# Grouped attention: 1280 of a unit's 1857 softmax columns traded by DMA instead of 1024, with new orders of step on all engines

## The reference

```
q = (latents @ Wq).reshape(b, q_len, N_KV_HEADS, N_GROUPS, HEAD_DIM)     # 32 heads of 128, 4 key heads
k = (hidden_states @ Wk).reshape(b, kv_len, N_KV_HEADS, HEAD_DIM)        # kv_len = 256 + 1601 = 1857
v = (hidden_states @ Wv).reshape(b, kv_len, N_KV_HEADS, HEAD_DIM)
scores = jnp.einsum('bqhgd,bkhd->bhgqk', q, k) * scale
attn = jax.nn.softmax(scores.astype(jnp.float32), axis=-1).astype(q.dtype)
out = jnp.einsum('bhgqk,bkhd->bqhgd', attn, v)
```

## Time and profile before

| what | value |
|---|---|
| median of three runs | 3167.3 us (3165.0 to 3168.3) |
| the profiled execution | 3163.82 us |
| its span, first to last instruction | 3162.1 us |
| granted TensorE clock over the span | 0.983 |
| busy: PE, PEld, DVE, ACT, POOL | 95%, 84%, 66%, 56%, 28% |

### The profile page before, as it was taken

The page is one execution under the profiler, slowest core; times in us unless marked ns, Lnnn a source line. Parts: engine busy times, 40 slices in busy tenths (PEclk is TensorE's granted clock), DMA queues, the critical chain, the costliest instruction groups (busy, mean ns, idle before and its releaser), DMA issues. The chain is left out here.

```text
span 3162.1 us, 53842 instructions
## 1 busy us (share of the span) xinstructions
PE 3008.4 (95%) x18405; PEld 2670.3 (84%) x18405; DVE 2076.8 (66%) x3217; ACT 1761.0 (56%) x3357; POOL 889.4 (28%) x725
## 2 busy tenths in 40 slices
PE   8999998999999999999999999979979899999886
PEld 8888887799999999899998999978857788888675
DVE  3333333688888888788887888864454466667576
ACT  3322344566766666666666666652243466556363
POOL 0000121344444444344444444442200021111234
PEclk9999999899999999999999999999989899999999
DMA  7665595776777767677767777546746511110387
GB/s 250 215 217 200 200 294 204 146 161 160 164 163 157 162 159 162 152 162 159 160 157 158 159 161 158 138 130 232 237 161 229 182 30 41 33 35 28 124 302 263
DMA packets 395364, 522.17 MB, mean 165 GB/s; under 512 B 35356, under 2 KB 292684, under 8 KB 395112
## 3 DMA queue, kind: packets, MB, share of 16 engines
q1 hardware_dynamic: 392552, 510.57, 59.2%
q0 software_dynamic: 2560, 8.39, 0.8%
HBM read 238.15 MB, written 146.46 MB: 122 GB/s over the span
## 5 line engine op out<-in xcount | busy, mean ns | idle before, releaser
L707 POOL TENSOR_TENSOR a_t_lo<-a_turned,a_t_hi 128x512 fp32r<-128x512 f32 x512 | 648.8, 1288 | 941.4 <-ACT a_t_hi L836 941.4
L827 ACT ACTIVATE a_probs<-a_ps_s,a_neg_max 128x1024 f32<-128x1024 f32 (+1 forms) x512 | 529.3, 1034 | 476.4 <-DVE a_neg_max L879 473.6
L872 DVE TENSOR_REDUCE a_half_max<-a_ps_s 128x1 f32<-128x1024 f32 (+1 forms) x512 | 570.7, 1115 | 191.1 <-PE a_ps_s L724 186.9
L722 PE MATMUL a_ps_s<-a_k_buf,a_q_buf 128*128 128x512 f32 (+1 forms) x1024 | 420.6, 411 | 18.0 <-ACT a_probs L827 11.8
L723 PE MATMUL a_ps_s<-a_k_buf,a_q_buf 128*128 128x512 f32 (+1 forms) x1024 | 386.6, 378 | 0.0
L724 PE MATMUL a_ps_s<-a_k_buf,a_q_buf 128*128 128x512 f32 (+1 forms) x1024 | 385.5, 376 | 0.0
L908 DVE TENSOR_TENSOR a_x_lo<-a_ps_x,a_x_hi 128x512 fp32r<-128x512 f32 (+1 forms) x512 | 314.2, 614 | 107.4 <-ACT a_x_hi L845 107.4
L454 DVE TENSOR_TENSOR p_out<-p_ps_j,p_out 128x512 fp32r<-128x512 f32 (+3 forms) x196 | 153.0, 780 | 327.4 <-ACT p_out L383 327.4
L898 DVE STREAM_TRANSPOSE a_turned<-xn 128x512 f32<-128x512 f32 x512 | 357.5, 698 | 1.5 <-POOL a_t_lo L707 1.5
L383 ACT ACTIVATE p_out<-p_ps_j 128x512 fp32r<-128x512 f32 (+3 forms) x196 | 142.1, 725 | 340.2 <-PE p_ps_j L288 340.2
L722 PE MATMUL a_ps_o<-a_t_hi,a_v_buf 128*128 128x256 f32 x1024 | 298.8, 292 | 5.6 <-issue 3.0
(11 more groups left out here) (383 smaller groups left out, 7001.1 us busy)
## 6 DMA issues: line engine op xcount, KB each, us to landing
xn<-a_probs SPq DMA_DIRECT2D x1024, 128.0 KB, 3.4
a_q_all<-p_out SPq DMA_DIRECT2D x64, 512.0 KB
a_q_buf<-a_q_all SPq DMA_DIRECT2D x128, 256.0 KB, 3.3
a_k_buf<-a_k_all SPq DMA_DIRECT2D x64, 464.5 KB, 4.0
a_v_all<-p_out SPq DMA_DIRECT2D x56, 512.0 KB
d_w_raw<-e_wt_all SPq DMA_DIRECT2D x31, 768.0 KB, 5.8
a_k_all<-p_out SPq DMA_DIRECT2D x48, 384.0 KB
a_v_buf<-a_v_all SPq DMA_DIRECT2D x64, 256.0 KB
```

The lines of the kernel that those rows point to most:

```text
L707: pool.tensor_tensor(t_lo[:, slot, :, :], turned[:, slot, :, :], t_hi[:, slot, :, :].bitcast(F32), ALU.subtract).then_inc(t_done, 1)
L722: pe.matmul(o, w_hi, m_hi, start=first, stop=False)
L827: act.activation(probs[j][u.a][:, lo:hi], s_flat[:, lo:hi], ACT.Exp, bias=neg_max[:, j:j + 1], scale=SCALE, accum_out=half_sum[:, bass.ds( ...
L872: dve.reduce_max(half_max[:, half:half + 1], s_flat[:, lo:hi], AX.X).then_inc(max_done, 1)
```

## The change

RUN goes from 256 to 320 columns. So 1280 columns are traded instead of 1024, and 577 are plain instead of 833: a unit has five turned pairs and three plain pairs (two full ones and the single tile of 65 keys) instead of four and four. RING goes to 5, PRING to 3. The buffer of the traded columns no longer fits twice into `xn`; its second half is a tile of its own. The fourth run (columns 960 to 1279) now holds columns of both halves, so SP waits for the second half's exponentials before it issues that run. In each engine's step the work of the fourth plain pair leaves, that of a fifth turned pair enters, and some places are swapped.

```
-    RUN = 256
+    RUN = 320
-    RING, PRING, XBANKS = 4, 4, 2
+    RING, PRING, XBANKS = 5, 3, 2
-            traded = xn[:, :, :].rearrange("p t d -> p (t d)")[:, 0:2 * QT * TURNED].rearrange("p (a j g r) -> p a j g r", a=2, j=QT, g=RUNS)
+            traded = [xn[:, :, :].rearrange("p t d -> p (t d)")[:, 0:QT * TURNED].rearrange("p (j g r) -> p j g r", j=QT, g=RUNS),
+                      sb("traded1", [P, QT, RUNS, RUN])]
                     for c in range(RUNS):
-                        sp.dma_start(traded[SQ * c:SQ * (c + 1), u.a, j, :, :], probs[j][u.a][:, RUN * c:RUN * (c + 1)]
+                        if c == RUNS - 1:
+                            sp.wait_ge(probs_done, 4 * u.n + 2 * j + 2)
+                        sp.dma_start(traded[u.a][SQ * c:SQ * (c + 1), j, :, :], probs[j][u.a][:, RUN * c:RUN * (c + 1)]
...
                     low(l, 3)
+                    low(l, 4)
                     low(w, 0)
...
                     turn_plain(l, 1)
-                    weigh_plain(z, 3)
+                    weigh_turned(z, 3)
                     scores(v, 0, 0)
                     turn_plain(l, 2)
                     scores(v, 0, 1)
-                    weigh_turned(z, 3, last=True)
-                    turn_plain(l, 3)
+                    weigh_turned(z, 4, last=True)
                     weigh_turned(l, 0, first=True)
...
                     exponentials(u, 0, 0)
-                    plain_high(w, 3)
+                    turned_high(w, 2)
                     exponentials(u, 0, 1)
-                    turned_high(w, 2)
                     turned_high(w, 3)
+                    turned_high(w, 4)
                     plain_high(v, 0)
...
                     turn_traded(l, 3)
                     maximum(v, 1, 0)
-                    plain_low(l, 3)
+                    turn_traded(l, 4)
                     maximum(v, 1, 1)
                     negate_maximum(v, 1)
                     plain_low(w, 0)
```

More of the change, by code:

```diff
@@ L526, in grouped_attention_block @@
     VPIECES = sum(len(p) for p in VALUE_PIECES)
-    assert QT == 2 and len(CHUNKS) == 4 and HPG == 8 and TURNED <= 2 * BANK and TBLOCKS % 2 == 0 and WIDTH % 2 == 0
+    assert QT == 2 and len(CHUNKS) == 4 and HPG == 8 and (RUNS - 1) * RUN <= 2 * BANK and TPAIRS == 5 and PPAIRS == 3 and TBLOCKS % 2 == 0 and WIDTH % 2 == 0
     assert PLAIN % 2 == 1 and TPAIRS * HEADS % RING == 0 and PPAIRS * HEADS % XBANKS == 0 and PPAIRS * HEADS % PRING == 0
@@ L898, in turn_traded @@
                     dve.transpose(turned[:, slot, :, :].rearrange("p k (q r) -> p k q r", r=SQ),
-                                  traded[:, u.a, :, :, 2 * SQ * p:2 * SQ * (p + 1)].rearrange("p j g (k r) -> p k (j g) r", k=2)
+                                  traded[u.a][:, :, :, 2 * SQ * p:2 * SQ * (p + 1)].rearrange("p j g (k r) -> p k (j g) r", k=2)
                                   ).then_inc(turn_done, 1)
```

## The result

The changed kernel takes 3218.1 us (median of 3 runs, 3212.6 to 3233.6) against 3167.3 before: ratio 1.0175, interval 1.0143 to 1.0206. It is slower, where faster was forecast. The profiled execution took 3212.6 with a span of 3210.9.

The account below looks back on a forecast made before the run. It took the chain through ACT to bound the loop body and PE's own work the first batch; loop body -2, straight line -9, end +1, together -10, gave 3157 us, range 3140 to 3184 (forecast's own 3148 to 3164).

Parts of the forecast that it names:

- The chain: Each loop's sequence from scores through maximum and exponentials to next scores; in the loop body, loop A -0.21, loop B +0.19.
- One sign: First batch: the second score matmul would now also stand 0.39 us behind the accumulator read's end.
- part (4): PE's work outside the chain, straight-line first batch: loop A -0.39, loop B +0.12, a unit -0.27; worth nothing in loop body.
- Rival 2, ACT late: Loop B: fifth high part, plain high part and exponentials run late in every unit; 3189 at the far end, chance 0.15.
- The disputed x: Loop B: time from DVE's end of the fifth turn to ACT's start; taken as 0.13 us, far end 0.39.
- Rival 1: PE is the bound everywhere and all its saving comes through: 0.44 a unit, time 3111, chance 0.10.
- part (6): DMA and SP: share 0.71 to about 0.81, later trades hidden by 2.5 us of slack, 0 for output store and query load.
- its 0 for the query load: SP's queue: the new wait ahead of the fourth run costs the query load queued behind it nothing.
- rival 3: Trades land late: from 2.5 us more delay on, each 0.3 us stalls DVE's first turn; 38 in all, 3195, chance 0.05.
- 2.5 us of slack hide it: Second trade of a unit lands about 1525.5, 3.4 us after issuing; the first turn needing it comes at 1528.

Follow-up runs that it names:

- experiment 3: Kernel before, its engine order untouched, with the changed kernel's 320-column trades and SP's new wait ahead of the fourth run: 3169.9 us.
- experiment 7: Changed kernel, same bytes and packets, each run written to all 128 partitions: 3155.6 us; to 64 of one half: 3189.8; to every second partition: 3160.3.
- experiment 4: Kernel before, its first trade of a unit made to wait for DVE's last plain low part: with 320-column trades 3205.8 us, with 256-column trades 3172.5.

## Why the prediction was wrong

**The chain: right.** In undisturbed loops nearly everything came out as worked out. The ends of the accumulator reads on ACT in the loop body:

```profile
1506.37 0.19 ACT L830 ACTIVATION_READ_ACCUMULATOR a_probs<-a_ps_s,a_neg_max  x1
...
1512.46 0.19 ACT L830 ACTIVATION_READ_ACCUMULATOR a_probs<-a_ps_s,a_neg_max  x1
...
1518.34 0.19 ACT L830 ACTIVATION_READ_ACCUMULATOR a_probs<-a_ps_s,a_neg_max  x1
```

The second matmuls follow 0.39, 0.40 and 0.40 later (1506.95, 1513.05, 1518.93), as in the earlier trace rows. Loop A takes 5.98 and 5.88, forecast 5.87; loop B 6.10, forecast 6.15. In the first batch the second matmuls show both loops:

```profile
705.31 0.40 PE L727 MATMUL a_ps_s<-a_k_buf,a_q_buf 128*128 128x512 f32 x1
...
711.36 0.39 PE L727 MATMUL a_ps_s<-a_k_buf,a_q_buf 128*128 128x512 f32 x1
...
716.97 0.39 PE L727 MATMUL a_ps_s<-a_k_buf,a_q_buf 128*128 128x512 f32 x1
```

Loop B 6.05, loop A 5.61; forecast 6.02 and 5.65. One sign did not come: at the end of loop B the second matmul still stands 0.45 behind the read there (medians of units 5 to 29), not 0.39, so PE's own work holds that loop a little. Where the crowding was removed (all partitions), a unit came out 0.27 shorter in the first batch, exactly the -0.27 of part (4), and 0.04 in the loop body, forecast 0.02. The last is in part luck: by the medians of that kernel loop A fell from 6.17 to 5.95 and loop B rose from 5.95 to 6.09, -0.08 together, and the longer loops where the loop of 32 steps begins anew, which the prediction did not have, took a part of it back.

**Rival 2, ACT late: not so.** Loop B's second maximum does start behind the turn, and ACT is in time:

```profile
1521.43 0.70 DVE L901 STREAM_TRANSPOSE a_turned<-a_traded 128x512 f32<-128x512 f32 x1
1522.05 0.98 DVE L875 TENSOR_REDUCE a_half_max<-a_ps_s 128x1 f32<-128x833 f32 x1
1523.07 0.21 DVE L882 TENSOR_SCALAR a_neg_max<-a_half_max 128x1 f32<-128x1 f32 x1
```

```profile
1522.16 0.63 ACT L839 ACTIVATE a_t_hi<-a_turned 128x512 fp32r<-128x512 f32 x1 [1.65 <-DVE a_turned L901]
1522.70 0.58 ACT L848 ACTIVATE a_x_hi<-a_ps_x 128x512 fp32r<-128x512 f32 x1
1523.41 1.12 ACT L830 ACTIVATE a_probs<-a_ps_s,a_neg_max 128x1024 f32<-128x1024 f32 x1
```

The disputed x is 1522.16 - 1522.13 = 0.03, and the exponentials start 0.13 after the negation's end, 1523.28. It was close: ACT's last high part ends at 1523.28 too. Rival 1 is out as well: loop B did not get shorter.

**The step that failed is part (6),** its 0 for the query load above all, and with it the "Against" of rival 3, "0.81 is not full".

- *"In proportion the share goes from 0.71 to about 0.81."* It went to 0.95 or 0.96 (experiment 3, at before's pace). The packets of a trade became not 25% dearer but some two thirds: packets of 1024 B took 73.1 ns on average before, those of 1280 B 122.7. (The 73.1 holds query, value and output transfers of the same packet size too.) The fastest twentieth is nearly in proportion (up to 46 and 55 ns); the rest is crowding in 32 partitions (experiment 7). The packet records of before had shown it already: in trades that began with nothing else under way, packets took 47 to 49 ns while the first run was alone, and 75 to 106 once runs overlapped. I read one share over 380 us instead of these.
- *"2.5 us of slack hide it."* The landing took 4.9 to 5.2 us in the median, not 3.4, and runs behind a backlog far longer.
- *"0 for the output store and query load queued behind it."* This is the term that cost the time. The 0 was worked out for the new wait ahead of the fourth run alone. The later start itself was foreseen (1515.4 instead of 1512.54, 2.86 later; measured 2.87), but I gave it a slack up to the first turn that needs the trade, and none was worked out for the query load that is last in SP's queue. That load landed 6.6 us after its issue instead of 3.2, and PE waited 40.6 us for it. Against the kernel before, some 40 of the 51 us by which units 2 to 126 take longer in the profiled runs lie at the one place in eight of those 15 waits, and 8 where the loop of 32 steps begins anew.
- The two delays were weighed apart, and apart they cost 5 and 5 to 7 us. Together they cost 40 (experiment 4). Rival 3 had the family of the mechanism, late transfers, but only DVE's turns as its place (they did wait 16 us for trades), and a chance of 0.05.

The changed kernel is 12 us slower than before with both delays, although its chains are shorter. That its units, where they run free, come sooner and ask for the same bytes in less time would explain that; it is argued, not shown. The trades also start 2.9 us later here and 2.6 there, and the value loads into 32 partitions carry 320 KB here and 256 KB there; what of the 12 us that makes is open too.

## What to carry to other kernels

When a change lets transfers start later and makes them longer, follow the queue of the issuing engine to its last member and work out that one's slack, with the landing times of a busy stretch and not the median of a quiet one. A DMA share is not a measure of that: 0.99 went with the lowest time where the queue started early, and 0.95 with 51 us of loss where it started 2.9 us late. Before moving transfers, look for the instruction that frees their buffer: taking the fifth turn ahead of a maximum, in idle time of DVE, gave 66 us against the changed kernel.

## What the runs showed of the hardware

**Which partitions a transfer is written to decides what its packets cost.** 1280 B packets: 122.7 ns into partitions 32c to 32c + 31, 115.5 into 0 to 63 or 64 to 127, 59.0 into every second partition, 59.1 into all. The Trainium skill (SBUF — State Buffer, Door 1: The DMA port swizzle) states that partitions 0 to 31 and 0 to 63 both reach the same 8 of 16 ports; by that rule 64 neighbours should do no better than 32 and every second partition as well as all 128, and the runs agree. That two runs that follow each other lie in different halves gave nothing (120.7 ns against 121.4).

**One wait of PE cost half as much again as its length.** After the 2.87 us without a matmul the next ones took 0.63 us instead of 0.40. The windows of the changed kernel around it, columns as above (a packet counts whole where it starts, so that a short window can have a share over 1):

```profile
1524.40:1527.60 3.20, 0.35 (x3) 0.15 (x2) 1.90 (x3) 2.27 (x6) 0.47 (x1) 1.00 1.12 218
1527.60:1530.00 2.40, 2.38 (x6) 1.92 (x7) 0.00 (x0) 0.63 (x1) 2.03 (x2) 0.54 1.12 170
1530.00:1532.00 2.00, 2.00 (x9) 1.62 (x9) 1.23 (x1) 0.38 (x1) 0.00 (x0) 0.70 1.13 187
1532.00:1534.00 2.00, 2.00 (x19) 2.00 (x18) 1.63 (x3) 0.10 (x1) 0.00 (x0) 1.00 1.12 176
```

The granted clock is 0.54 and 0.70 after the wait, the lower of its two levels (1.2 GHz) for most of it, and back at full speed by 1532. Loop A behind the wait lasts from 1528.07 to 1535.49, 7.42 instead of 5.9 to 6.0: some 1.5 us more, about half of the wait itself. Five score matmuls in it at a pitch of 0.43 instead of 0.23 are 1.0 of the 1.5.
